# Cross-attention with a quantised layer behind it: scores of three batches from 32 rows per head, in three rounds of four heads

## What is computed

```
q = (layernorm(x) @ W_q.T)   k = (ctx @ W_k.T)   v = (ctx @ W_v.T)      # 16 heads of 32
scores = einsum('bhqd,bhkd->bhqk', q, k) / sqrt(32)
e = exp(clip(scores, -50, 50));  attn = e / sum(e)
x = x + (einsum('bhqk,bhkd->bhqd', attn, v) joined) @ W_o.T  (rows masked)
x = x + quantised_matmul(layernorm(x), rhs)
```

## Time and profile before

| | |
|---|---|
| median of three runs | 1717.78 us |
| the profiled execution | 1718.7 us, of which its span 1716.7 us |
| mean granted TensorE clock | 0.995 |
| busy: PE, DVE, ACT, POOL | 98%, 87%, 77%, 8% |
| DMA engines | 66% on the queue that carries the tensors |
| the twelve segments of the change | from 135.7 us to about 1331 us of the span |

### The profile page before, as it was taken

How to read it: one execution, slowest core, us unless ns; L and a number is a source line. 1 busy time by engine, 2 the same in 40 slices (tenths; PEclk the granted TensorE clock), 3 DMA queues, 4 the chain that set the end, 5 groups by cost and what they waited for, 6 DMA issues and landing times.

```text
span 1716.7 us, 29869 instructions
## 1 busy us (share of the span) xinstructions
PE 1677.0 (98%) x10418; PEld 1013.5 (59%) x10448; DVE 1489.9 (87%) x1705; ACT 1314.5 (77%) x1730; POOL 133.8 (8%) x75
## 2 busy tenths in 40 slices
PE   8999999999999999999999999999999899999997
PEld 7996655655565665665666565666656344444445
DVE  5657888888898989899898999989899789999996
ACT  5557888888887778878787787787877678787883
POOL 0000000000001111010110101111010010001001
PEclk9999999999999999999999999999999999999999
DMA  7787556566676665756756676665756878988952
GB/s 255 225 232 191 142 144 151 150 168 167 150 174 147 160 179 149 212 129 174 180 136 175 158 186 161 159 176 135 208 135 163 207 169 203 223 175 202 218 146 80
DMA packets 235636, 295.90 MB, mean 172 GB/s; under 512 B 28249, under 2 KB 142425, under 8 KB 234969
## 3 DMA queue, kind: packets, MB, share of 16 engines
q1 hardware_dynamic: 232264, 288.69, 66.2%
q10 hardware_dynamic: 3216, 5.24, 1.1%
HBM read 201.59 MB, written 92.00 MB: 171 GB/s over the span
## 4 chain that ended last, share of the span: by engine, by line
PE 81%; DVE 6%; DMA 5%; ACT 5%; issue 2%; SPq 1%; POOL 0%; ACTq 0%; DVEq 0%
PE tile L965 24%; PE wsum L1002 24%; PE scores L987 21%; ACT probs L1251 4%; DVE acc L1554 4%; PE scores L1151 3%; PE scores L965 2%; PE tile L1034 1%; PE tile L1151 1%; DMA o_parts<-sums 1%; DMA row_lo<-o_parts 1%; PE tile L1114 1%; PE tile L1091 1%; PE scores L626 1%; DMA den_c<-denoms 1%
## 5 line engine op out<-in xcount | busy, mean ns | idle before, releaser
L1251 ACT ACTIVATE probs<-scores 128x1024 f32<-128x1024 f32 x939 | 914.7, 1026 | 208.0 <-PE scores L987 168.9
L1554 DVE TENSOR_TENSOR acc<-acc,probs 128x2048 f32<-128x2048 f32 x439 | 1003.4, 2286 | 40.3 <-ACT probs L1251 25.8
L1002 PE MATMUL wsum<-probs,v_sb 128*32 128x512 f32 x4096 | 493.4, 599 | 0.0
L987 PE MATMUL scores<-q_stack,k_stack 128*128 128x512 f32 x1536 | 444.5, 409 | 2.5 <-ACT probs L1251 1.7
L987 PEld LDWEIGHTS scores<-q_stack,k_stack 128*128 128x128 f32 x1536 | 265.1, 188 | 212.8 <-ACT probs L1251 121.2
L1002 PEld LDWEIGHTS wsum<-probs,v_sb 128*32 128x32 f32 x4096 | 107.2, 109 | 243.6 <-issue 229.8
L1656 POOL TENSOR_TENSOR rstd<-var_eps,minus_half 128x1 f32<-128x1 f32 x48 | 106.0, 2208 | 1187.3 <-DVE var_eps L1448 1187.3
L1554 DVE TENSOR_TENSOR acc<-probs 128x2048 f32<-128x2048 f32 x32 | 73.4, 2293 | 56.5 <-PE tile L1034 51.2
L1151 PE MATMUL scores<-q_stack,k_stack 128*128 128x512 f32 x342 | 110.4, 424 | 10.5 <-ACT probs L1251 10.5
L965 PE MATMUL tile<-ctx_hi,wk_hi 128*128 128x256 f32 x412 | 116.5, 283 | 0.0
L965 PE MATMUL tile<-ctx_hi,wk_lo 128*128 128x256 f32 x412 | 116.1, 282 | 0.0
(11 more groups left out here) (247 smaller groups left out, 1990.2 us busy)
## 6 DMA issues: line engine op xcount, KB each, us to landing
k_stack<-k_parts SPq DMA_DIRECT2D x312, 256.0 KB, 7.6
q_stack<-q_parts SPq DMA_DIRECT2D x124, 256.0 KB, 7.3
v_sb<-v_parts SPq DMA_DIRECT2D x80, 256.0 KB, 7.4
v_parts<-v_stage SPq DMA_DIRECT2D x64, 256.0 KB, 5.0
raw<-ctxT SPq DMA_DIRECT2D x27, 512.0 KB, 6.6
k_parts<-stage_hi SPq DMA_DIRECT2D x96, 128.0 KB, 4.5
k_parts<-stage_lo SPq DMA_DIRECT2D x96, 128.0 KB, 2.4
x_in<-x SPq DMA_DIRECT2D x33, 256.0 KB, 4.8
```

Of the source, the lines that this page charges most:

```text
L987: last = nc.tensor.matmul(scores[:, h, :], k_stack[:, kt // 4, h, (kt % 4) * P:(kt % 4 + 1) * P], q_stack[:, qb, h, :], start=True, stop=True)
L1002: last = nc.tensor.matmul(wsum[DH * h:DH * h + DH, :], v_sb[:, kt, DH * h:DH * h + DH], probs[:, n % RING, h, :], start=(kt == 0), stop=(k ...
L1251: nc.scalar.activation(probs[:, slot % RING, 2 * pair:2 * pair + 2, :], score_banks(seg, slot, pair), ACT.Exp, scale=1.0 / math.sqrt(DH)). ...
L1554: nc.vector.tensor_tensor(acc[:, :, :], other, probs[:, slot % RING, :, :], ALU.add).then_inc(sems["add_done"], 1)
```

## The change

Keys and queries of the first three batches are no longer replicated. `stacked(j)` says which group of heads still is: the last batch's. For the others `load_k` and `load_q` copy the planes as they stand, two transfers of 128 rows instead of four of 32 rows by four heads: head h lies in rows 32h to 32h + 32, the hi part in place 0 and the lo part in place 1 of the same buffers. The scores of a head are three matmuls over its 32 rows, accumulated in its bank: hi by hi, lo by hi, hi by lo. The fourth product, lo by lo, which the stacked form summed as well, is left out. The twelve matmuls of a slot go in three rounds of four heads. The waits for `exp_done` stand ahead of heads 0 and 2 of the first round, and `scores_full` is given behind heads 1 and 3 of the third. The last batch (`final_scores`) is as before.

```diff
--- before.py
+++ after.py
@@ -277,9 +277,9 @@
     **{f"x_loaded{n}": (lambda g, n=n: 16 * (g.has("load_x", n) + g.has("load_x", n + 2) + (g.s == 0))) for n in range(2)},
     "raw_loaded0": lambda g: 16 * g.has("load_raw", 2), "raw_loaded1": lambda g: 16 * (g.has("load_raw", 1) + (g.s == 0)),
     "orows_loaded": (0, 0, 32), "xr_loaded": (0, 0, 32),
-    **{f"k_loaded{n}": (lambda g: 64 * g.b * (1 + g.final)) for n in range(4)},
+    **{f"k_loaded{n}": (lambda g: 128 if g.final else 32 * g.b) for n in range(4)},
     **{f"v_loaded{n}": (lambda g: 16 * g.b * (1 + g.final)) for n in range(4)},
-    "q_loaded0": (0, 64, 0), "q_loaded1": (0, 64, 0),
+    **{f"q_loaded{n}": (lambda g: 64 if g.final else 32 * g.b) for n in range(2)},
 
     **{f"{part}_stored{n}": (lambda seg, n=n: 0 if not seg.a else 16 * STAGED // 4 if not seg.b else 16 * STAGED // 2 if n < 2 else 0)
        for part in ("hi", "lo") for n in range(4)},
@@ -706,9 +706,17 @@
                 if n >= FULL + 3:
                     add_rows(pool, nc.gpsimd.tensor_tensor, n - 3)
 
+        def stacked(j):
+
+            return j >= (B - 1) * G
+
         def load_k(eng, j, quarter):
 
             src = k_parts[j, :, :, quarter * 4 * P:(quarter + 1) * 4 * P]
+            if not stacked(j):
+                for part in range(2):
+                    eng.dma_start(k_stack[:, quarter, part, :].bitcast(F32), src[part]).then_inc(sems[f"k_loaded{quarter}"], 16)
+                return
             for part in range(2):
                 for twice in range(2):
                     at = 64 * twice + 32 * part
@@ -718,6 +726,10 @@
         def load_q(eng, j, qb, half=None):
 
             src, at = q_parts[j, :, :, qb * QB:(qb + 1) * QB], qb if half is None else half
+            if not stacked(j):
+                for part in range(2):
+                    eng.dma_start(q_stack[:, at, part, :].bitcast(F32), src[part]).then_inc(sems[f"q_loaded{at}"], 16)
+                return
             for r in range(4):
                 eng.dma_start(q_stack[DH * r:DH * r + DH, at, :, :].bitcast(F32),
                              src[r // 2].rearrange("(h d) t -> d h t", d=DH)).then_inc(sems[f"q_loaded{at}"], 16)
@@ -978,15 +990,19 @@
 
                     qb, kt = divmod(n, KT)
                     if kt == 0:
-                        ct.wait(pe, f"q_loaded{qb}", 64)
+                        ct.wait(pe, f"q_loaded{qb}", 32)
                     if qb == 0 and kt % 4 == 0:
-                        ct.wait(pe, f"k_loaded{kt // 4}", 64)
-                    for pair in range(2):
-                        ct.wait(pe, "exp_done", 2 * n + pair - 1)
-                        for h in (2 * pair, 2 * pair + 1):
-                            last = nc.tensor.matmul(scores[:, h, :], k_stack[:, kt // 4, h, (kt % 4) * P:(kt % 4 + 1) * P],
-                                                    q_stack[:, qb, h, :], start=True, stop=True)
-                        last.then_inc(sems["scores_full"], 1)
+                        ct.wait(pe, f"k_loaded{kt // 4}", 32)
+                    keys = slice((kt % 4) * P, (kt % 4 + 1) * P)
+                    for term, (k_part, q_part) in enumerate(((0, 0), (1, 0), (0, 1))):
+                        for h in range(G):
+                            if not term and h % 2 == 0:
+                                ct.wait(pe, "exp_done", 2 * n + h // 2 - 1)
+                            rows = slice(DH * h, DH * h + DH)
+                            last = nc.tensor.matmul(scores[:, h, :], k_stack[rows, kt // 4, k_part, keys], q_stack[rows, qb, q_part, :],
+                                                    start=(term == 0), stop=(term == 2))
+                            if term == 2 and h % 2:
+                                last.then_inc(sems["scores_full"], 1)
 
                 def sums_of(n):
 
```

## The result

The changed kernel takes 1748.97 us (median of four runs, 1747.37 to 1749.23) against 1717.79 us beside it (1716.49 to 1719.31). The ratio is 1.0179, 95% interval 1.0162 to 1.0197: slower by 31 us, where 10.7 was forecast. The sign is the forecast's and the time lies in the range; the size is three times what the sum gave.

The account below looks back on a forecast made before the run. TensorE was taken as the bound (98% busy, 81% of the chain). Terms 10.6 - 2.3 - 2.4 + 4.8 = +10.7 us on 1718.7 gave 1729.4, as run median 1728.5; own range 1700 to 1760 (chance 0.60), overall 1690 to 1785.

Parts of the forecast that it names:

- loads barred: Rival, score rounds: no weight load under a running matmul of the same rows, steps 0.34; +63, 1780; chance 0.12.
- loads in a row: Rival, score blocks: twelve weight loads of 0.11 one after another, block 1.32 long; +234, 1952; chance 0.08.
- no overlap: Rival, score blocks: matmuls on different rows run one by one, eight more steps of 0.23; +710, 2430; chance 0.03.
- The switches, 0.10 each and 0.40 a cycle: Array shape changes on PE, even block to pieces and pieces to odd block: drain and open load, 0.10 each.
- free switches: Rival, around the pieces: rows-to-whole shape changes cost nothing, 119 long cycles save 0.30 more; 1685, faster; chance 0.17.
- The loops, 3.01 unstalled and 2.79 from a release on: PE and ScalarE handover: next head 2 comes 3.01 after an unwaiting block's start, or 2.79 after a waiting head 2's release.
- EO becomes 0.35 (head 2 to the block's last): 119 long cycles, even to odd block (EO), pieces of length L: 0.35 + 0.33 + L + 0.10 + 0.10; cycles -2.4 us.
- short cycle: Cycle with L below 1.87 (K, Q, V or X pieces alone): 5.58 against 5.34, +0.24, 44 times, +10.6 us.
- Middle cycles: 25 cycles with two V or O thirds (L 1.87): about 5.68 against 5.78, -0.09 each, -2.3 us.
- ScalarE's split of the context, +4.8: ScalarE's gap between blocks falls to 0.85; the 1.06 split doesn't fit, twice in twelve segments: 24 x 0.2 us.
- The loads, "at most -1 us": k_stack and q_stack transfers halved, some 37.7 MB less: costed at nothing, at most -1 us.
- if round two can't pass the waiting head 2: High end of the forecast's range, score blocks: the loop would be 3.01 everywhere, +29 us.

## Why the prediction came out as it did

- *Four heads side by side, three steps instead of four:* right. The second round starts 0.33 behind the first (its load lies open), the third 0.23 behind the second, 0.01 within one, 0.58 from first to last. The rivals with loads barred (1780), loads in a row (1952) and no overlap (2430) fell at the first block of the trace. The Trainium skill (TensorE: Matmul & The Clock Gate, Part 3) has a load overlap matmuls only where the row group differs; here the third round reloads the rows on which the second is running, and starts 0.23 us behind it as with whole loads; the trace decides against it.
- *The switches, 0.10 each and 0.40 a cycle:* right, 0.39 measured. The rival of free switches falls.
- *The loops, 3.01 unstalled and 2.79 from a release on:* right. The first measures 2.99 to 3.00; of the second, ScalarE starts 0.79 after the release (656.49 after 655.70) and its gap is 0.84.
- ***"EO becomes 0.35 (head 2 to the block's last)"*: this step failed.** The 0.35 is what heads 0 and 1 have left when head 2 is let go. Heads 2 and 3 have all three rounds ahead of them then: 0.34 and 0.23, which is 0.57. The prediction has their second round at T+0.34 itself, for ScalarE's side, and doesn't carry it on to the third for PE's. In the trace, 655.70 to 656.27. A stalled long cycle is 0.57 + 0.33 + L + 0.20 + 3.01 = 4.11 + L instead of 3.89 + L; measured 6.45 with L of 2.36, thus 4.09 + L. Before it was 3.91 + L.
- *The same slip in the short cycle.* I let both ways be ScalarE's loop (2.79 + 2.79). After a stalled odd block PE still has its 0.57 and then the sums: 0.57 + 2.18 = 2.75, so a cycle takes 3.01 + 2.75 = 5.76; measured 5.74, forecast 5.58, before 5.34 (2.46 + 2.88; 5.35 in the cycle of the earlier trace rows). The next even block, too, begins so late that it doesn't wait at all, which the timeline shows (1.01 long). Middle cycles whose even block stalls (17 of 25) measure 5.95 to 5.97 in place of 5.68, the eight others, in the first batch, 5.75 to 5.77; the mean is 5.90.
- *The sum again with this one step mended:* short 44 x 0.42 = 18.5; middle 25 x 0.17 = 4.3, as if all stalled; of the 119 long ones 79 stall at the even block and come to 79 x 0.20 = 15.8, and 40 don't (their even block follows a denominator or a short cycle), 40 x -0.05 = -2.0. That is 36.6, against 31.4 measured in these classes (19.3, 3.0 and 9.1); the rest of the difference is in the stalled long ones, at 0.16 each, in the eight middle ones, and in the two long ones that the loads made shorter by 2.0. The forecast had 5.9 for the three.
- *ScalarE's split of the context, +4.8:* the trace doesn't bear it out. Of 23 splits in the twelve segments 17 are followed by the next exponentials within 0.02 us of their release, and six, five of them in the first batch, by ones 0.53 late; before, 13 were 0.22 to 0.97 late. No run was made on it.
- *The loads, "at most -1 us":* mis-sized. They measured -3.6 (0.9979). The row that I read, 0.8 us of waits for k_stack in all, was not the place; 2.6 of it lie in two segments, where PE's gaps had other names, and the rest isn't placed.
- *Left open:* the last stage. It took 385.8 us before, 382.7 in the changed kernel, 390.4 in the kernel with 96 rows (in the slowest of its eleven runs), and 384.3 to 386.7 in all other runs, with nearly the same code there. A wait for a transfer of denominators took 3.4 us before and 1.7 in the changed kernel; the rest isn't placed. So the 3.1 us that the changed kernel gains there are not ascribed to the change: the other runs speak for chance.
- *Range and rivals:* the 1749 lies in the forecast's own range (1700 to 1760), which reached up for another reason, "if round two can't pass the waiting head 2". That bound, 3.01 everywhere, is priced at 29 us on top of the sum, 1757. It isn't what happened: the second round of heads 0 and 1 is held until head 2 is let go, but then starts 0.09 behind the release and 0.25 ahead of heads 2 and 3's. That the range held the result is in part luck. The sign "PE's busy share lower" didn't show either, 98% both times, since the matmuls of heads 0 and 1 cover the stall.

## What to carry to other kernels

Where one engine releases another in pieces, running the parts side by side makes all pieces ready together: a shorter block can hand over later, and here that was worth more than the time saved. Write such a loop down for both sides from each wait on, with everything that the waiting parts still have to do, and not with what their neighbours have left. A short test tells whether the handover is the loss: shorten the work on the other side of the handover by a few tenths and see which of the two kernels gains.

## What the runs showed of the hardware that I had not expected

- Matmuls on different groups of 32 rows need not start in the order of the program: in the kernel with the first pair ahead, head 2's first matmul started 0.01 us after head 0's, and 0.33 ahead of two that stand before it in the program; twelve matmuls took 0.97 to 0.99 us in all three orders. A wait is not passed: in the block at 655.46 the load of head 2 that waits held the second round of heads 0 and 1 behind it until 655.79, 0.09 after its release.
- Twelve loads of 32 rows by 128 columns took 0.54 us in such a block, beside the matmuls.
- In the kernel with one round PE was busy some 95% of the twelve segments, with no pause over 2.6 us, and the granted clock fell to the lower level (1.2 GHz) 18 times, for a mean of 0.96 to 0.98.
- A contraction over 96 rows between others over 128 costs no switch: the blocks of that kernel are 0.80 and 0.70 from first to last start, as before.
